# Four transposed tiles of a fused graph-network kernel: from TensorE transposes to 32x32 block turns and DMA, in a new order

## What is computed

```
L0: 8 heads: softmax(q k / sqrt(16) + adj * W_e[h], where adj) v, then @ W_o.T
L1: x_conv = relu(bn(conv17(relu(bn(conv1(x))))) + x);  A = exp(-dist(s)) * adj;  x_nmp = A @ relu(x @ w_msg.T + b)
    r, z = sigmoid(gates of [x_conv, x_nmp], x); n = tanh(..);  out = (1 - z) * n + z * x
L2: u = adj * exp(e_i + f_j);  out = (u / rowsum u) @ h,   h = x @ W.T + b
L3: 4 heads: softmax(leaky(e_i + e_j), where adj > 0) @ h,   h = x @ W
```

## Time and profile before

| | |
|---|---|
| median of 3 runs | 1429.45 us (1429.4 to 1431.82) |
| the profiled execution: time, span | 1432.08 us, 1430.3 us |
| busy: PE, DVE, ACT, POOL | 1352.1 us (95%), 1191.3 (83%), 1188.4 (83%), 663.1 (46%) |
| DMA | 46.86 MB, queue of SP 9.8% of the 16 engines' span |

### The profile page before, as it was taken

How to read it: one execution, slowest core, us unless ns; L and a number is a source line. 1 busy time by engine, 2 the same in 40 slices (tenths; PEclk the granted TensorE clock), 3 DMA queues, 4 the chain that set the end, 5 groups by cost and what they waited for, 6 DMA issues and landing times.

```text
span 1430.3 us, 40514 instructions
## 1 busy us (share of the span) xinstructions
PE 1352.1 (95%) x13178; PEld 1075.1 (75%) x13267; DVE 1191.3 (83%) x3407; ACT 1188.4 (83%) x4353; POOL 663.1 (46%) x1014
## 2 busy tenths in 40 slices
PE   4799999999999999999999999999999999999964
PEld 3577788877778887777888777788877778887642
DVE  6568888888888888888888888888888888886763
ACT  3867888889888888998888899888889988887654
POOL 1133445554444555444455544445554444555532
PEclk7899999999999999999999999999999999999986
DMA  3100110011111001111100111111011111100000
GB/s 117 38 31 31 31 31 17 16 39 38 39 38 39 25 16 39 38 38 39 39 29 12 39 39 38 38 39 34 6 39 39 38 39 38 33 8 16 9 15 23
DMA packets 23825, 46.86 MB, mean 33 GB/s; under 512 B 2753, under 2 KB 2754, under 8 KB 23490
## 3 DMA queue, kind: packets, MB, share of 16 engines
q1 hardware_dynamic: 23618, 44.27, 9.8%
HBM read 35.88 MB, written 8.39 MB: 31 GB/s over the span
## 4 chain that ended last, share of the span: by engine, by line
PE 78%; DVE 10%; POOL 5%; issue 4%; ACT 3%; DVEq 0%; POOLq 0%; ACTq 0%
PE B L591 18%; PE B L689 14%; PE B L499 12%; PE B L537 5%; PE B L558 4%; DVE B L1353 4%; DVE x L1326 3%; POOL rstd L376 3%; PE B L808 2%; PE B L523 2%; PE B L788 2%; PE B L754 2%; PE B L581 2%; PE B L665 2%; PE B L683 2%
## 5 line engine op out<-in xcount | busy, mean ns | idle before, releaser
L995 ACT ACTIVATE e<-B,nm 128x128 f32<-128x128 f32 x1024 | 363.9, 385 | 12.5 <-DVE nm L1361 12.0
L499 PEld LDWEIGHTS B<-ident,e 128*128 128x128 f32 x1536 | 187.0, 144 | 104.3 <-issue 75.7
L499 PE MATMUL B<-ident,e 128*128 128x128 f32 x1536 | 230.0, 281 | 9.2 <-ACT e L1151 3.9
L995 ACT ACTIVATION_READ_ACCUMULATOR e<-B,nm 128x1 f32 x1024 | 231.9, 226 | 0.0
L1353 DVE SCALAR_TENSOR_TENSOR B<-an,rowb,mask 128x512 f32<-128x512 f32 x256 | 194.2, 794 | 19.0 <-ACT pT L1004 9.5
L1151 ACT ACTIVATE e<-l,nm 128x128 f32<-128x128 f32 x512 | 198.9, 400 | 10.0 <-DVE nm L1582 9.9
L1361 DVE TENSOR_REDUCE nm<-B 128x4 f32<-128x512 f32 x256 | 166.5, 683 | 35.0 <-PE B L537 34.8
L1004 ACT ACTIVATE pT<-B 128x512 f32<-128x512 f32 x256 | 157.9, 617 | 44.5 <-PE B L499 41.3
L373 POOL TENSOR_TENSOR veps<-meanv,eps 128x4 f32<-128x4 f32 x128 | 41.8, 326 | 328.9 <-DVE meanv L1320 328.8
L376 POOL TENSOR_TENSOR rstd<-veps,neghalf 128x4 f32<-128x4 f32 x128 | 139.7, 1092 | 10.0
L1582 DVE TENSOR_REDUCE nm<-l 128x4 f32<-128x512 f32 x128 | 87.0, 679 | 41.9 <-ACT l L1141 41.9
(11 more groups left out here) (201 smaller groups left out, 3471.1 us busy)
## 6 DMA issues: line engine op xcount, KB each, us to landing
xt<-in_x_t SPq DMA_DIRECT2D x32, 256.0 KB, 3.1
an<-in_adj_n SPq DMA_DIRECT2D x32, 256.0 KB, 2.7
xn<-in_x_n SPq DMA_DIRECT2D x32, 256.0 KB, 3.3
at<-in_adj_t SPq DMA_DIRECT2D x32, 256.0 KB, 3.2
out_x<-xo SPq DMA_DIRECT2D x32, 256.0 KB, 3.5
wm<-in_mats SPq DMA_DIRECT2D x1, 1088.0 KB, 9.4
wm<-in_mats SPq DMA_DIRECT2D x1, 832.0 KB, 7.1
wm<-in_mats SPq DMA_DIRECT2D x1, 320.0 KB, 3.0
```

The costliest lines, as they stand in the source:

```text
L499: last = mm(g(dst, b), g(src, b), ident[:, :], is_transpose=True, start=(b == 0), stop=True, skip_group_check=True)
L995: last = fn(g(e0[:, h % 2, :], b), g(bank, b), ACT.Exp, bias=nm0[:, h % 4, b:b + 1], accum_out=sum0[s % 2][:, b, head(h):head(h) + 1])
```

## The change

The four tiles other than x1 no longer go through TensorE. VectorE turns each in 32x32 blocks (`v.transpose`), which leaves every block in the place that it had; SP writes the result to a buffer in HBM, waits until it has landed, and reads it back with the blocks exchanged, in four transfers, one for each 32 partitions, in runs of 32 floats (128 bytes). The sums are turned in one 128x32 piece, written in four small transfers, and read back once, each row spread over 16 partitions, so GpSimd's spread goes too. out3 is turned by VectorE straight from PSUM. x1 stays as it was. The three `keep_` copies of ScalarE, `spread_sums`, `sums_T`, `y_T`, `x3_T` and `out3_T` are gone. All five lists have a new order, and `rest_of_weights` comes at t == 2, after the masks of the first two groups. A group still takes eight steps of VectorE's list.

```diff
-STEPS = GROUPS + 16
+MOVED = 4 * DMA
+STEPS = GROUPS + 9
+            def write_blocks(s, done, sent, got, here, there):
+                wait(sp, q[got], MOVED * s)
+                sp.wait_ge(q[done], s + 1)
+                sp.dma_start(there[:, :], here[:, :]).then_inc(q[sent], DMA)
+            def read_blocks(s, sent, got, there, here):
+                sp.wait_ge(q[sent], DMA * (s + 1))
+                for c in range(4):
+                    sp.dma_start(here[32 * c:32 * c + 32, :].rearrange("r (b i j) -> r b i j", b=GB, i=4),
+                                 there.rearrange("(i r) (b c j) -> c r b i j", i=4, b=GB, c=4)[c]).then_inc(q[got], DMA)
+            def write_sums(s):
+                wait(sp, q["recT_got"], DMA * s)
+                sp.wait_ge(q["rbt_done"], s + 1)
+                for i in range(4):
+                    sp.dma_start(inv_mem.rearrange("h (b i j) -> i (h b) j", b=GB, i=4)[i],
+                                 recb[32 * i:32 * i + 32, :]).then_inc(q["rb_sent"], DMA)
+            def read_sums(s):
+                wait(sp, q["oT_ready"], s)
+                sp.wait_ge(q["rb_sent"], MOVED * (s + 1))
+                sp.dma_start(recT[:, :], inv_mem.unsqueeze(1).broadcast_to([H0, D0, GB * N])).then_inc(q["recT_got"], DMA)
...
             def step(t):
+                read_y(t - 4)
+                write_out3(t - 6)
+                load_at(t - 2)
                 load_xt(t)
+                load_xn(t - 1)
+                read_out3(t - 6)
                 load_an(t)
-                load_xn(t)
-                store(t - 8)
-                load_at(t - 1)
+                write_x3(t - 4)
+                read_x3(t - 4)
+                write_sums(t - 1)
+                read_sums(t - 1)
+                store(t - 9)
+                write_y(t - 3)
...
+            def turn_x3(s):
+                wait(dve, q["x3_sent"], DMA * s)
+                dve.wait_ge(ln_out[2], s + 1)
+                v.transpose(x3b[:, :], x3[s % 2][:, :]).then_inc(q["x3b_done"], 1)
+            def turn_out3(s, bank):
+                wait(dve, q["o3_sent"], DMA * s)
+                dve.wait_ge(q["pv3_ps"], s + 1)
+                v.transpose(o3b[:, :], bank[:, :]).then_inc(q["o3b_done"], 1)
...
-                if t == 3:
+                if t == 2:
                     rest_of_weights()
```

More of the change, by code:

```diff
@@ new lines, in write_out3, with read_out3, write_x3, read_x3 @@
+            def write_out3(s):
+                write_blocks(s, "o3b_done", "o3_sent", "o3_got", o3b, o3_mem)
+            def read_out3(s):
+                if not live(s):
+                    return
+                wait(sp, q["n3_done"], s)
+                read_blocks(s, "o3_sent", "o3_got", o3_mem, o3n)
+            def write_x3(s):
+                write_blocks(s, "x3b_done", "x3_sent", "x3T_ready", x3b, x3_mem)
+            def read_x3(s):
+                if not live(s):
+                    return
+                wait(sp, q["h3_ps"], s)
+                wait(sp, q["ej_ps"], s)
+                read_blocks(s, "x3_sent", "x3T_ready", x3_mem, x3T)
@@ L295, in store, with write_y, read_y @@
+            def write_y(s):
+                write_blocks(s, "yb_done", "y_sent", "y_got", yb, y_mem)
+            def read_y(s):
+                if not live(s):
+                    return
+                wait(sp, ln_out[1], s)
+                read_blocks(s, "y_sent", "y_got", y_mem, yn)
             def store(s):
@@ L561, in values @@
                 last.then_inc(q["pv_ps"], 1)
[L563 to L571, removed]
             def project_out(s, bank, users):
@@ L1488, in gru_out, with turn_y, stats1 @@
                 v.tensor_tensor(yT[:, :], zn[:, :], zx[:, :], ALU.add).then_inc(q["y_done"], 1)
-            def stats1(s, bank):
+            def turn_y(s):
+                if not live(s):
+                    return
+                wait(dve, q["y_sent"], DMA * s)
+                dve.wait_ge(q["y_done"], s + 1)
+                v.transpose(yb[:, :], yT[:, :]).then_inc(q["yb_done"], 1)
+            def stats1(s):
                 if not live(s):
@@ new lines, in step @@
+                edge_mask(t)
+                residual3(t - 6)
+                seed_edges(t, 0, B[7], (("g1_done", -3, 1, 1), ("tz_ready", -3, 1, 1),
+                    ("pT3_ready", -5, 4, 1), ("xc_ready", -3, 1, 1), ("exp_done", -1, 8, 1)))
+                row_max3(t - 5, 3)
+                norm2(t - 4)
+                turn_x3(t - 4)
+                seed_edges(t, 1, B[3], (("qT_ready", 0, 1, 1), ("tr_ready", -3, 1, 1),
+                    ("l3_done", -5, 4, 3), ("pT_ready", -1, 8, 3), ("pT_ready", -1, 8, 2),
+                    ("exp_done", -1, 8, 2)))
@@ new lines, in step @@
+                gru_out(t - 3)
+                sides(t - 2)
+                row_max(t, 0, B[7])
+                turn_y(t - 3)
+                turn_out3(t - 5, B[6])
+                row_max(t, 1, B[3])
+                aggr3(t - 6)
+                row_max(t, 2, B[0])
+                divide(t - 1, B[1])
+                invert_sums3(t - 5)
+                row_max(t, 3, B[5])
+                shared_to_phases(t - 2, B[4])
+                shared_to_halves(t - 2, B[4], B[7], (("exp_done", 2, 8, 1), ("g1_done", -1, 1, 1),
+                    ("tz_ready", -1, 1, 1), ("pT3_ready", -3, 4, 1), ("xc_ready", -1, 1, 1)))
```

588 lines of the change are left out of this document (266 added, 322 removed).

## The result

The changed kernel takes 1493.78 us, the median of 4 runs (1487.51 to 1496.11), against 1430.21 us for the kernel before on the same chip: a ratio of 1.0436, with a 95% interval of 1.0423 to 1.0448. It is slower by 4.4%, where I had forecast 1405 us and 1380 to 1450. The profiled execution took 1492.25 us.

What follows compares the result with a forecast made beforehand. TensorE's queue was taken as the bound: steps of 40.4 us instead of 41.65 give -35 us over 28 steps, start -3, end +13, so -25 on 1432.08 gives 1407, as median 1405 us; range 1380 to 1450.

Steps and rivals of the forecast that it cites:

- In the steady part time is worth what TensorE's queue is worth, until VectorE fills.: Steady steps of 41.65 us: TensorE, 99% busy, sets the time; VectorE has 4.85 us idle a step.
- 1.75 us a step: TensorE's queue: transposes of four tiles leave it, 0.44 us each, which sets a floor of 39.9 us a step.
- 10 + 4 x 3 = 22 us of 40: it fits.: SP's queue in a step: 10 us of issues plus four waits of 3 us for writes to land.
- The tightest is x3T.: x3's way to TensorE's matmul: 13.9 to 16.5 us against a slot of 15.4; the middle, 15.2, just fits.
- The sums are similar: Sums' way to the division: 9.5 us of VectorE work, then write 1.7, read 3.1 and the queue behind x3's reads.
- One issue takes 0.36 us ... so 25 x 0.4 = 10 us.: SP's issue time: 0.36 us for 128 pieces, taken as 0.4 for each of 25 transfers a step.
- I add 0.5 us for small waits.: Steady step: 0.5 us added to the 39.9 us floor because slots are close, giving 40.4 us a step.
- Small pieces at 16 ns: Reads of moved tiles: 128-byte pieces cost 16 ns each, taken from col's row, so a tile reads in 2.0 us.
- The rival that they cost as large ones: Tile reads: pieces at 95 ns, 12 us a tile, step 48.9 us, 1660 us in all; chance 0.04.
- Block transpose at 0.60 us: VectorE: three large turns at 0.60 us plus 0.15 for the small one, 1.95 us a step, 38.7 us busy.
- The rival in which VectorE becomes the bound: VectorE: turns at 0.97 us, 39.8 us busy, steps of 40.8 to 41.3 us, 1416 to 1430 us; chance 0.12.
- The rival "transfers are late": x3T comes after its slot and TensorE stands; at 2 us late 41.9 us a step, 1453 us; chance 0.20.

Runs made afterwards that it cites:

- b_sums: Kernel before in its own order, only layer 0's inverted sums turned on VectorE and moved through memory by SP: 1430.3 us, ratio 1.0001.
- h_before: Kernel before with one line moved, edge_mask(t - 9) ahead of divide3(t - 15) on VectorE: 1422.2 us, ratio 0.9942.
- a_neither: Changed kernel without the moves and without the three large turns (output not the reference's): 1416.0 us, ratio 0.9904 to the kernel before.
- h_neither: Changed kernel without moves and three large turns, message_bias placed ahead of stats3 and invert_sums on VectorE (output not the reference's): 1390.4 us, ratio 0.9722.
- c_sums_first: Changed kernel with SP issuing the four writes of the turned sums ahead of the four reads of x3T: 1497.4 us, ratio 1.0472.
- i_pool_msg: Changed kernel with the sums' write (one DMA) and read issued by GpSimd, and message_bias ahead of stats3 and invert_sums: 1448.2 us, ratio 1.0112.
- c_pool_sums: Changed kernel with the sums' write (one DMA for four) and read issued by GpSimd, no longer by SP: 1447.8 us, ratio 1.0121.

## Why the prediction was wrong

- **"In the steady part time is worth what TensorE's queue is worth, until VectorE fills."** The first failed step. It has two holes. TensorE at 99% lay on a loop with VectorE's program, so work taken out at one place of its queue was worth nothing (b_sums), and one mask moved on VectorE was worth 8 us (h_before). And the new order had its own loop at 41.1 us (a_neither, h_neither). Of the 1.75 us a step that were to come off, 0.5 came in a_neither. The 1.75 was itself too much: 4 x 0.44 is right for the rows, but TensorE's work fell by 1.2; why is open.
- **"10 + 4 x 3 = 22 us of 40: it fits."** The step that cost the sign. The sum was nearly right: from the first write to the last landing it is 25 us. But I asked whether the queue fits in a step, and not who waits at its end: out3's read is the last of the round trips, and its tile releases VectorE's work that leads to the next x3. 26 us and VectorE's 18 us between o3n and x3 make 43.9.
- **"The tightest is x3T."** x3T was first in the queue and in time: TensorE waited for it 17 us in the whole run, nearly all of it at the ends. "The sums are similar", "y ... about 9 us for about 7" and "out3 over 10 us" were each counted from the tile's turn, as if the queue were free then. y was turned by 660.7, written at 662.09, landed at 666.05 and read back after 670. The slots were right and the starts wrong. My check was right in one thing: with one more write ahead of it (c_sums_first) x3T was late, by 1.7 us a step.
- **"One issue takes 0.36 us ... so 25 x 0.4 = 10 us."** Mis-sized: 0.65 for each of the 12 reads of 512 pieces, 0.49 for each of the sums' writes; SP's issues in a step are 14 us. I had named this as what would make me wrong; it has its part, since only issues that stand in the loop count. Those of the reads, the sums and the store did; those of the four loads did not (three are hidden behind out3's write, the fourth comes after the reads), 1.5 us a step.
- **"I add 0.5 us for small waits."** The term on the floor of 39.9 us came out at 3.2 us: the step is 43.1. VectorE was to idle 1.7 us a step (40.4 - 38.7) and idles 4.2 of 43.5.
- **Small pieces at 16 ns.** Right, and a little high. From 654.2 to 658 us the changed kernel moves only pieces of 128 bytes, those of x3T and the sums:

```profile
DMA packets 1848, 0.23 MB, mean 61 GB/s; under 512 B 1848, under 2 KB 1848, under 8 KB 1848
q1 hardware_dynamic: 1848, 0.23, 38.6%
```

  38.6% of 16 engines over 3.8 us is 12.7 ns a piece. A quarter tile of x3T landed 2.2 to 3.6 us after its issue, median 2.4, where I had 1.7 to 2.9. The rival that they cost as large ones, and with it the 19-fold rule of the Trainium skill that I had set beside it ("VectorE: DVE Perf Modes", The three transpose paths), doesn't show for blocks in runs of 128 bytes; no run here used the crossbar path, so the factor itself stays untested.
- **Block transpose at 0.60 us.** 0.71 long and 0.63 to 0.64 from start to start; VectorE's work is 39.35 us a step against 38.7. It didn't matter: without the turns the time is the same. The rival in which VectorE becomes the bound did not occur, though 18 us of VectorE's program stand on the loop.
- **The ends.** -3 at the start was +7.2: the first mask does start at 12.14 instead of 19.51, but VectorE then waits for the queries, and the first steps have the round trips exposed; without the moves the start is 207.6 us, so they cost 4.7 of the 7.2. +13 at the end was +14.8, but by luck: without the moves the end is 175.4 us, so they cost 23 there, and the rest of the change, which I had at nothing, gave 9 back.
- **The rival "transfers are late"** was the right sign with the wrong place. It put the wait on x3T and asked for a write of x3 of 3.5 us and pieces of 25 ns. Neither was needed: x3's and out3's writes took 2.1 and 2.4 us (medians), y's 4.2, and pieces of 12.7 ns are slow enough when the round trips stand in one line. x3T's way does bind, at 40.6 us, once the rest is relieved (i_pool_msg).
- **"Sum 13.9 to 16.5 us."** The items of x3T's way, as listed, add up to 13.7 to 16.3; the slip of 0.2 us changes nothing.

## What to carry to other kernels

Before pricing a move off the busiest engine, follow its waits, small ones too, around one whole step: where a wait of an engine that is 99% busy closes a loop through another engine's in-order program, only what shortens the loop counts. Before adding round trips to a DMA queue, write its program out as a line with its waits, and add the work between the last landing and the first write of the next step: that sum must be below the step, not the queue alone. One DMA for four and a second queue gave back 46 of the 64 us here.

## What was not expected of the hardware

- SP's issue time isn't one number: 0.33 to 0.43 us for a load of 256 KB in long rows, 0.36 for col, 0.42 (median) for a sums' write of 32 pieces, 0.59 for the same write in one DMA of 128, 0.65 for 64 KB in 512 pieces, four in a row 2.60 us.
- A DMA issued by GpSimd took 0.80 us (the sums' write) and 0.62 us (their read) of its program in c_pool_sums; their median landings were 2.6 and 3.7 us.
- With the loop through the queue the steps are uneven: the last 21 of the changed kernel take 42.4 to 45.1 us, where those of the kernel before take 41.45 to 41.65, all but one.
